# Starting addresses of the expert stage's tiles: a right-end spacer of 480 bytes, and two small tensors joined to others

## The chip, the cores and the metric

One core of one Trainium2 chip. The metric is device microseconds of the whole program, the median of several runs. A run of the same program is repeated to within some tenths of a per cent; three runs of the kernel before gave 1493.5, 1497.95 and 1489.89 us.

## The reference

A decoder layer on x of 8 batches x 256 tokens x 512 features, float32:

```python
x = x + attn(layernorm(x))            # 16 heads, keys masked to 26 first and 64 last positions
x = x + long_conv(ctx, ctx, layernorm(x), ssm_kernel, D)   # 32 heads of 8 x 8 products, causal convolution
x = x + moe(layernorm(x))
# moe: E = 12 experts, top 3 of a softmax router, 512 -> 1280 -> 512
for e in range(E):
    sel = top_idx == e; mask = sel.any(-1)
    w_e = sum(where(sel, ew, 0)) / max(sel.sum(), 1)
    h = relu(x @ w1[e] + b1[e]);  h = h @ w2[e] + b2[e]
    out = out + mask * (w_e * h)
phi = sigmoid(relu(out.mean(axis=1) @ Wp1 + bp1) @ Wp2 + bp2)
return out * (1.0 - (phi > 0.7) * 0.8)
```

Inputs and outputs are float32. Products are made of three float32r matmuls each: every factor is split in a rounded high part and a low part, and hi*hi + hi*lo + lo*hi is summed.

## The kernel before, in words

The program runs four functions one after the other: `attention` (0 to some 300 us), `convolution` (to some 494 us), `route` (to some 523 us) and `experts` (to the end). Each has one instruction stream per engine, in an order written out by hand, tied together by semaphores. No planner takes part.

`route` sorts the 2048 x 3 pairs of token and expert into NTILE = 59 tiles of 128 tokens, so that each tile belongs to one expert, and leaves tables: `gidx` (rows to gather), `sidx` (rows to add to), `wt`, `eid`, `tstart_i`, `wexp`. Meanwhile the first expert's weights arrive in `w_lo` by four DMAs and ScalarE rounds them into `w_hi`.

`experts` goes through the 59 tiles. For a tile, GpSimd gathers 128 rows of the normalised x from DRAM (`gather`, L1797 to L1800, into `xg`; the first two, L1849 and L1852, stand before the loop), TensorE transposes them (L1947), ScalarE and GpSimd make `xf`, `xh`, `xl` (L1877, L1878, L1806), TensorE makes the first product in column chunks of 512, 512 and 256 (L1962, L1963, L1967: `ps_h`), ScalarE copies it to `h` (L1884), TensorE transposes it (L1975), ScalarE applies bias and relu into `h` and rounds into `hh` (L1893, L1897), GpSimd makes `hl` (L1810), TensorE makes the second product (L1985, L1986, L1989: `ps_y`), ScalarE scales into `y` (L1903), GpSimd adds the bias (L1820) and adds the rows to `acc` in DRAM by an indirect DMA (L1835). TensorE's order for a tile is: transposes of h, first product of the next tile, transposes of x for the tile after that, second product.

The weights of the next expert are loaded beside this by SyncE in 20 chunks of [128, 512] into the four buffers of `stage` (L1640), and VectorE splits each into `w_hi` and `w_lo` (L1685, L1687). Before each half of the chunks VectorE waits for TensorE's last use of the buffer and does a one-column addition into `turn` (L1728, L1732). GpSimd does such one-column additions into columns 0 to 4 of `tick` (`settle`, L1794).

At the end SyncE reads the sums of all tiles but two back from `acc` (L1666, four DMAs of 1 MB), VectorE adds them in pairs (L1752) and TensorE pools them (L1996); when the last tile is added, eight DMAs of 512 KB fetch `acc` (L1671), VectorE combines (L1783) and eight DMAs store (L1675).

All operands of this stage lie in SBUF at addresses that follow from the order of allocation. A tile on the left side begins where the one before it ended, rounded up to 32 bytes; a tile on the right side is laid downwards from 229344. By that arithmetic the byte addresses within a partition are these, with the remainder by 512 in brackets: `gidx` 19616 (160); `si` 22912, `tick` 22944, `turn` 22976, `b1_now` 23008; `xf` 23072 (32), `xh` 25120 (32), `xl` 27168 (32), `h` 29216 (32), `hh` 34336 (32), `hl` 39456 (32), `y` 44576 (32), ending at 48672; from the right `w_hi` 147424 (480), `w_lo` 65504 (480), `stage` 57312 (480), `b2_sb` 53216 (480), `gi` 53184 (448), `xg` 49088 (448). In `attention` the weights `wq_hi` to `wo_lo` begin at remainder 384, and `xs` and `qe` too; the transposed rows that its matmuls load beside them begin at 0 (`xT_hi` 176640, `xT_lo` 180736) and at 416 (`oT_hi` 215456, `oT_lo` 217504). Every row, chunk and buffer inside these tiles is a multiple of 512 bytes long where TensorE or a DMA starts a run in it, so that the remainder is the same for all of them.

Of the kernel before, what the change touches and what calls it, by code (L numbers as in the profile page):

```python
# [6 lines left out]
F32 = mybir.dt.float32  # L7
# [3 lines left out]
U32 = mybir.dt.uint32  # L11
ACT = mybir.ActivationFunctionType
ALU = mybir.AluOpType
AX_X = mybir.AxisListType.X

P = 128
B, S, D = 8, 256, 512
# [32 lines left out]
NTILE = NT * TOPK + (E * (P - 1)) // P  # L50
# [1489 lines left out]
def experts(nc, cst, w_hi, w_lo, stage, stage_in, split_done, wcat, b2, b2_sb, b2_in, b2_ready, b1_sb, xnd, x2d, x2,  # L1540
# [6 lines left out]
    gidx, sidx, wt, eid, tstart_i, wexp = tabs  # L1547
    gi, xg, gi_ready, g_in = first
    tile_f, cnt, ps_t = book
    o, o_in, end_small, small_in = end  # L1550
    with ExitStack() as ctx:
        def sb(name, shape, dt=F32):
            return ctx.enter_context(nc.sbuf_tensor(name, shape, dt))
# [4 lines left out]
        def sem(name):  # L1558
            return ctx.enter_context(nc.semaphore(name))

        si = sb("si", [P, 2], U32)
        tick = sb("tick", [P, 5])
        turn = sb("turn", [P, 1])
        b1_now = sb("b1_now", [P, KF])
        xf = sb("xf", [P, KD * P])
        xh = sb("xh", [P, KD * P], F32R)
# [51 lines left out]
        tabs_ready = sem("tabs_ready")  # L1618
# [60 lines left out]
        def _(dve):  # L1679
# [14 lines left out]
            v = nc.vector  # L1694
# [3 lines left out]
            expert, used_, tok_, to_ = (tile_f[:, i] for i in range(4))  # L1698
# [3 lines left out]
            note(v.tensor_scalar(tok_, m_tile, float(P), -1.0, ALU.mult, ALU.add))  # L1702
            note(v.tensor_tensor(tok_, tok_, m_place, ALU.add))
            note(v.tensor_scalar(tok_, tok_, 0.0, None, ALU.max))
            v.tensor_copy(gidx[:], tok_).then_inc(tabs_ready, 1)
            dve.wait_ge(gi_ready, 2)
            lower(0)
            lower(1)
# [16 lines left out]
                lower(q)  # L1725
            with dve.Fori(1, E) as e:
                dve.wait_ge(h_done, first_tile(dve, e - 1, 3))
                nc.vector.tensor_tensor(turn[:], cst[:, 0:1], cst[:, 0:1], ALU.add)  # L1728
                for c in range(N1):
                    split(e, c)  # L1730
                dve.wait_ge(y_done, first_tile(dve, e - 1, 1))
                nc.vector.tensor_tensor(turn[:], cst[:, 0:1], cst[:, 0:1], ALU.add)  # L1732
                for c in range(N1, NCHUNK):
                    split(e, c)
                dve.wait_ge(b2_in, 16 * e + 16)
                b2_w = view(b2_sb[:], (e % 2) * D, [[1, D]])
                nc.vector.tensor_tensor(b2_w, b2_w, view(wexp[:], e, [[0, D]]), ALU.mult).then_inc(b2_ready, 1)
# [313 lines left out]
def decoder_layer(nc, out, **a):  # L2051

    with ExitStack() as ctx:
        def sb(stack, name, shape, dt=F32):
            return stack.enter_context(nc.sbuf_tensor(name, shape, dt))

        cst = sb(ctx, "cst", [P, NCONST])
        tabs = (sb(ctx, "gidx", [P, NTILE], U32), sb(ctx, "sidx", [P, NTILE], U32), sb(ctx, "wt", [P, NTILE]),
                sb(ctx, "eid", [1, NTILE], I32), sb(ctx, "tstart_i", [1, E], I32), sb(ctx, "wexp", [P, E]))
        b1_sb = sb(ctx, "b1_sb", [P, E * KF])  # L2060
        kpad = nc.dram_tensor("kpad", (SH, KPAD), F32, kind="Internal").ap()
        x2d = nc.dram_tensor("x2d", (NT * P, D), F32, kind="Internal").ap()
        xnd = nc.dram_tensor("xnd", (NT * P, D), F32, kind="Internal").ap()
        acc = nc.dram_tensor("acc", (NT * P + P, D), F32, kind="Internal").ap()
        with ExitStack() as mid:
            ranked = (sb(mid, "prob", [P, NT, E]), sb(mid, "rank", [P, NT, E]), sb(mid, "col", [P, 2, NT]))
            with ExitStack() as early:
                xs = sb(early, "xs", [P, NT, D])
                qe = sb(early, "qe", [P, LB * B * SH * CH])
                dve_step = ctx.enter_context(nc.semaphore("dve_step"))  # L2070
                exps = [ctx.enter_context(nc.semaphore(n)) for n in ("exp_in", "exp_out")]
                count = [0]

                def moved(steps=None):
                    if steps is not None:
                        count[0] = steps.base + steps.n
                    return count[0]

                front = sb(early, "front", [P, (TPB + 8) * D])
                n_kv, n_cc = LB * B * NPAIR, LB * B * CE  # L2080
                sizes = [n_kv] * AHEAD + [n_cc] * 2 + [D] * AHEAD
                parts = [front[:, sum(sizes[:i]):sum(sizes[:i + 1])] for i in range(len(sizes))]
                ahead = (parts[AHEAD + 2:], parts[AHEAD:AHEAD + 2], parts[:AHEAD],
                         [early.enter_context(nc.semaphore(f"toe_in{i}")) for i in range(NTOE)],
                         [early.enter_context(nc.semaphore(f"cc_in{i}")) for i in range(2)],
                         early.enter_context(nc.semaphore("kv_ready")))
                attention(nc, xs, cst, a["x"], a["L0_attn_Wq"], a["L0_attn_Wk"], a["L0_attn_Wv"], a["L0_attn_Wo"],
                          a["L0_attn_bq"], a["L0_attn_bk"], a["L0_attn_bv"], a["L0_attn_bo"], a["consts"], qe,
                          a["L0_xattn_ssm_kernel"], a["L0_xattn_D"], kpad, a["ctx_rev"], front, ahead, dve_step, moved)
                res = sb(early, "res", [P, LB * B * S])  # L2090
                convolution(nc, xs, cst, qe, res, a["ctx_rev"], kpad, ranked, a["L0_ffn_Wr"], a["L0_ffn_br"],
                            a["L0_ffn_b1"], b1_sb, x2d, xnd, acc, ahead, dve_step, moved, exps)
            with ExitStack() as late:
                w_hi = late.enter_context(nc.sbuf_tensor("w_hi", [P, 2, WS], F32R, side="right"))
                w_lo = late.enter_context(nc.sbuf_tensor("w_lo", [P, 2, WS], F32R, side="right"))
                x2_in = late.enter_context(nc.semaphore("x2_in"))
                x2 = w_hi[:, 0, 0:NT * D].bitcast(F32).rearrange("p (t d) -> p t d", d=D)
                o = w_lo[:, 0, 0:NT * D].bitcast(F32).rearrange("p (t d) -> p t d", d=D)
                spare = w_lo[:, 0, NT * D:WS].bitcast(F32)
                wp1, bp1, wp2, bp2 = (a[f"L0_ffn_{n}"] for n in ("Wp1", "bp1", "Wp2", "bp2"))  # L2100
                PH = wp1.shape[1]
                KP = PH // P
                gate = (spare[:, 0:KD * PH].rearrange("p (k n) -> p k n", k=KD), spare[:, KD * PH:KD * PH + KP],
                        spare[:, KD * PH + KP:KD * PH + 2 * KP], spare[:, KD * PH + 2 * KP:KD * PH + 2 * KP + 1])
                end_small = ((gate[0], wp1.rearrange("(k p) n -> p k n", p=P)), (gate[1], bp1), (gate[2], wp2),
                             (gate[3], bp2.partition_broadcast(P)))
                end = (o, [late.enter_context(nc.semaphore(f"o_in{b}")) for b in range(B)], end_small,
                       late.enter_context(nc.semaphore("small_in_e")))
                with ExitStack() as busy:
                    def right(name, shape, dt=F32):  # L2110
                        return busy.enter_context(nc.sbuf_tensor(name, shape, dt, side="right"))

                    stage = right("stage", [P, NSTAGE, WC])
                    b2_sb = right("b2_sb", [P, 2, D])
                    stage_in = [busy.enter_context(nc.semaphore(f"stage_in{i}")) for i in range(NSTAGE)]
                    split_done = busy.enter_context(nc.semaphore("split_done"))
                    b2_in = busy.enter_context(nc.semaphore("b2_in"))
                    b2_ready = busy.enter_context(nc.semaphore("b2_ready"))
                    first = (right("gi", [P, 2], U32), right("xg", [P, 2, D]), busy.enter_context(nc.semaphore("gi_ready")),
                             [busy.enter_context(nc.semaphore(f"g_in{i}")) for i in range(2)])  # L2120
                    book = (view(stage[:], 0, [[NTILE, 4], [1, NTILE]]), view(stage[:], 4 * NTILE, [[E, 6], [1, E]]),
                            busy.enter_context(nc.psum_tensor("ps_td", [P, 3, 512], F32)))
                    route(nc, cst, ranked, w_hi, w_lo, a["wcat"], a["L0_ffn_b2"], b2_sb, b2_in, first, tabs, book, dve_step, moved, exps)
                    experts(nc, cst, w_hi, w_lo, stage, stage_in, split_done, a["wcat"], a["L0_ffn_b2"], b2_sb, b2_in,
                            b2_ready, b1_sb, xnd, x2d, x2, x2_in, acc, first, end, gate, out, tabs, book, dve_step, moved)
# [55 lines left out]
```

## Time and profile before

| | |
|---|---|
| median of three runs | 1493.5 us |
| profiled execution, its time | 1495.83 us |
| profiled execution, its span | 1494.1 us |
| TensorE busy, share of the span | 1379.5 us, 92% |
| GpSimd busy | 842.6 us, 56% |
| VectorE busy | 819.8 us, 55% |
| ScalarE busy | 698.1 us, 47% |
| mean granted clock of TensorE | 0.953 |

The busy time of TensorE says only that a matmul was in flight, since they overlap. The chain of work that ended last tells which of them set the time, and the table by stretches tells where the engine had nothing to do. PE is TensorE, DVE VectorE, ACT ScalarE, POOL GpSimd, SP SyncE; a q behind the name is the engine's sequencer, which issues DMAs.

### The profile page before, as it was taken

What the parts mean: (1) busy time and instruction counts of PE and PEld (TensorE: products, weight loads), DVE (VectorE), ACT (ScalarE), POOL (GpSimd) and SP (SyncE); (2) the same over time, 40 slices, a digit from 0 to 9 for tenths busy, and PEclk for the clock granted to TensorE, in tenths of its full rate; (3) what the DMA queues carried; (4) which work ended last, traced back from release to release, by engine and by line L of the source; (5) the groups of instructions that cost most, each with busy time, mean ns of one, the idle gap of its engine ahead of it and who ended that gap; (6) DMA issues with size and microseconds to landing.
All of it is one profiled execution on the core that took longest, in us unless ns stands there. A gap on an engine that the chain in (4) does not pass through costs nothing.

```text
span 1494.1 us, 27777 instructions
## 1 busy us (share of the span) xinstructions
PE 1379.5 (92%) x7868; PEld 1135.9 (76%) x7869; DVE 819.8 (55%) x1197; ACT 698.1 (47%) x1878; POOL 842.6 (56%) x955
## 2 busy tenths in 40 slices
PE   5899998799986279999999999999999999999994
PEld 3777776577765268888888888888888888888883
DVE  6788887599997884745264444647444452000013
ACT  3657666244554234454444544445444454444530
POOL 0456445244653067767576676767766666565640
PEclk9999998899997589999999999999999999999985
DMA  7000000253333335545254344445444443151146
GB/s 268 1 1 0 0 0 26 82 188 97 111 99 136 153 115 126 147 113 137 66 148 105 106 106 111 124 113 156 107 111 95 123 112 77 35 154 35 31 132 232
DMA packets 77576, 152.42 MB, mean 102 GB/s; under 512 B 9120, under 2 KB 13728, under 8 KB 77024
## 3 DMA queue, kind: packets, MB, share of 16 engines
q1 hardware_dynamic: 62496, 115.09, 24.2%
q0 software_dynamic: 14320, 35.40, 12.0%
q10 hardware_dynamic: 720, 1.44, 0.3%
q8 instruction: 21, 0.34, 0.1%
q14 instruction: 19, 0.16, 0.0%
HBM read 119.31 MB, written 32.59 MB: 102 GB/s over the span
## 4 chain that ended last, share of the span: by engine, by line
PE 62%; DMA 2%; DVE 0%; SPq 0%; issue 0%; ACT 0%; DVEq 0%; POOL 0%; POOLq 0%
PE ps_h L1962 9%; PE ps_h L1967 9%; PE ps_h L1963 9%; PE ps_y L1985 9%; PE ps_y L1986 9%; PE ps_y L1989 9%; PE ps_td L1975 4%; PE ps_xd L1947 2%; DMA w_lo<-acc 1%; PE ps_xd L1996 0%; DMA xg<-xnd,gi 0%; DMA acc<-y,si 0%; DVE w_lo L1783 0%; SPq L1671 0%; DVE w_lo L1752 0%
## 5 line engine op out<-in xcount | busy, mean ns | idle before, releaser
L1962 PE MATMUL ps_h<-w_hi,xh 128*128 x708 | 251.5, 367 | 1.5 <-ACT xh L1878 1.4
L1963 PE MATMUL ps_h<-w_lo,xh 128*128 x708 | 244.3, 356 | 0.0
L1687 DVE TENSOR_TENSOR w_lo<-stage,w_hi 128x512 f32 x220 | 226.6, 1030 | 28.6 <-DVE w_hi L1685 2.9
L1985 PE MATMUL ps_y<-w_hi,hh 128*128 x590 | 238.8, 405 | 0.0
L1986 PE MATMUL ps_y<-w_lo,hh 128*128 x590 | 233.6, 396 | 0.0
L1820 POOL TENSOR_TENSOR y<-y,b_sb 128x512 f32<-128x512 f32 x58 | 79.7, 1374 | 226.6 <-ACT y L1903 226.6
L1810 POOL TENSOR_TENSOR hl<-h,hh 128x1280 fp32r<-128x1280 f32 x59 | 180.9, 3067 | 17.9 <-ACT hh L1897 17.5
L1903 ACT ACTIVATE y<-ps_y,wt 128x512 f32<-128x512 f32 x59 | 40.6, 688 | 293.5 <-PE ps_y L1989 293.5
L1884 ACT ACTIVATE h<-ps_h 128x512 f32<-128x512 f32 x177 | 80.7, 527 | 196.5 <-POOL hl L1810 185.6
L1967 PE MATMUL ps_h<-w_hi,xl 128*128 x708 | 166.7, 357 | 0.0
L1893 ACT ACTIVATE h<-ps_td,b_now 128x128 f32<-128x128 f32 x590 | 159.0, 392 | 3.9 <-PE ps_td L1975 1.2
L1962 PEld LDWEIGHTS ps_h<-w_hi,xh 128*128 128x128 f32 x708 | 133.9, 189 | 24.5 <-issue 2.1
L1963 PEld LDWEIGHTS ps_h<-w_lo,xh 128*128 128x128 f32 x708 | 134.0, 189 | 20.3
L1989 PE MATMUL ps_y<-w_hi,hl 128*128 x590 | 147.5, 395 | 0.0
L1728 DVE TENSOR_TENSOR turn<-cst 128x1 f32<-128x1 f32 x11 | 2.7, 242 | 253.6 <-PE ps_h L1967 253.6
L1967 PEld LDWEIGHTS ps_h<-w_hi,xl 128*128 128x128 f32 x708 | 120.6, 188 | 21.4
L1989 PEld LDWEIGHTS ps_y<-w_hi,hl 128*128 128x128 f32 x590 | 110.3, 187 | 27.3
L1985 PEld LDWEIGHTS ps_y<-w_hi,hh 128*128 128x128 f32 x590 | 111.4, 189 | 24.9
L1986 PEld LDWEIGHTS ps_y<-w_lo,hh 128*128 128x128 f32 x590 | 111.3, 189 | 24.8
L1685 DVE CAST w_hi<-stage 128x512 f32 x220 | 126.5, 575 | 5.2 <-DMA stage<-in_wcat 4.3
L1835 POOL DMA_INDIRECT acc<-y,si x59 | 101.1, 1714 | 29.4 <-issue 14.9
L1742 DVE COPY xf<-w_lo 128x256 f32<-128x256 f32 x1 | 0.3, 295 | 181.3 <-POOL xl L1806 181.3
(256 smaller groups left out, 2647.6 us busy)
## 6 DMA issues: line engine op xcount, KB each, us to landing
stage<-in_wcat SPq DMA_DIRECT2D x220, 256.0 KB, 3.0
front<-in_ctx_rev SPq DMA_DIRECT2D x32, 192.0 KB, 2.4
w_lo<-in_wcat SPq DMA_DIRECT2D x4, 1280.0 KB, 11.7
acc<-added_c POOLq DMA_DIRECT2D x1, 4352.0 KB, 17.4
front<-kpad SPq DMA_DIRECT2D x16, 256.0 KB, 3.4
toe<-kpad SPq DMA_DIRECT2D x16, 256.0 KB, 3.6
x2d<-xs SPq DMA_DIRECT2D x16, 256.0 KB, 2.4
xnd<-xn_c SPq DMA_DIRECT2D x16, 256.0 KB, 2.0
```

Of the source, the lines that this page charges most:

```text
L1685: nc.vector.tensor_copy(hi, stage[:, c % NSTAGE]).then_inc(w_rounded, 1)
L1687: nc.vector.tensor_tensor(lo, stage[:, c % NSTAGE], hi.bitcast(F32), ALU.subtract).then_inc(split_done, 1)
L1810: nc.gpsimd.tensor_tensor(hl[:], h[:], hh[:].bitcast(F32), ALU.subtract).then_inc(hl_ready, 1)
L1835: pool.indirect_dma_start(acc, bass.IndirectOffsetOnAxis(ap=si[:, par:par + 1], axis=0), y[:, par], None, compute_op=ALU.add).then_inc(add ...
L1884: nc.scalar.activation(h[:, lo:hi], ps_h[:, c, 0:hi - lo], ACT.Copy).then_inc(h_evac, 1)
L1893: last = nc.scalar.activation(h[:, k * P:(k + 1) * P], ps_t[:, k // 4, (k % 4) * P:(k % 4 + 1) * P], ACT.Relu, bias=b1_now[:, k:k + 1])
L1962: nc.tensor.matmul(out, x_hi, part(w_hi, e, k * FF + lo, hi - lo), start=(k == 0), stop=False)
L1963: nc.tensor.matmul(out, x_hi, part(w_lo, e, k * FF + lo, hi - lo), start=False, stop=False)
L1967: last = nc.tensor.matmul(out, xl[:, k * P:(k + 1) * P], part(w_hi, e, k * FF + lo, hi - lo), start=False, stop=(k == KD - 1))
L1985: nc.tensor.matmul(ps_y[:], h_hi, part(w_hi, e, KD * FF + k * D, D), start=(k == 0), stop=False)
L1986: nc.tensor.matmul(ps_y[:], h_hi, part(w_lo, e, KD * FF + k * D, D), start=False, stop=False)
L1989: last = nc.tensor.matmul(ps_y[:], hl[:, k * P:(k + 1) * P], part(w_hi, e, KD * FF + k * D, D), start=False, stop=(k == KF - 1))
```

## The change

A tensor `tail` of 120 float32 (480 bytes) that nothing uses is allocated first on the right side, so that all below it moves down by 480 bytes. `gi` becomes the last two columns of `gidx`, and `turn` the sixth column of `tick`. The rows of `gidx` and `tick` still take 256 and 32 bytes, so nothing on the left side ahead of `tick` moves. By the same arithmetic: `b1_now` 22976, `xf` 23040 (0), `xh` 25088 (0), `xl` 27136 (0), `h` 29184 (0), `hh` 34304 (0), `hl` 39424 (0), `y` 44544 (0), ending at 48640; `w_hi` 146944 (0), `w_lo` 65024 (0), `stage` 56832 (0), `b2_sb` 52736 (0), `xg` 48640 (0); `gi` at 19852. No instruction, wait, loop or DMA is added or taken away, and none changes its shape.

```diff
-        tick = sb("tick", [P, 5])
-        turn = sb("turn", [P, 1])
+        tick = sb("tick", [P, 6])
+        turn = tick[:, 5:6]
...
-            v.tensor_copy(gidx[:], tok_).then_inc(tabs_ready, 1)
+            v.tensor_copy(gidx[:, 0:NTILE], tok_).then_inc(tabs_ready, 1)
...
-                nc.vector.tensor_tensor(turn[:], cst[:, 0:1], cst[:, 0:1], ALU.add)     # L1728, L1732
+                nc.vector.tensor_tensor(turn, cst[:, 0:1], cst[:, 0:1], ALU.add)
...
-        tabs = (sb(ctx, "gidx", [P, NTILE], U32), sb(ctx, "sidx", [P, NTILE], U32), sb(ctx, "wt", [P, NTILE]),
+        tabs = (sb(ctx, "gidx", [P, NTILE + 2], U32), sb(ctx, "sidx", [P, NTILE], U32), sb(ctx, "wt", [P, NTILE]),
...
             with ExitStack() as late:
+
+                late.enter_context(nc.sbuf_tensor("tail", [P, 120], F32, side="right"))
                 w_hi = late.enter_context(nc.sbuf_tensor("w_hi", [P, 2, WS], F32R, side="right"))
...
-                    first = (right("gi", [P, 2], U32), right("xg", [P, 2, D]), ...
+                    first = (tabs[0][:, NTILE:NTILE + 2], right("xg", [P, 2, D]), ...
```

## Rows read from the trace of the kernel before

**Rows 1.** The page's chain of work that ended last, by engine and by line.
```profile
PE 62%; DMA 2%; DVE 0%; SPq 0%; issue 0%; ACT 0%; DVEq 0%; POOL 0%; POOLq 0%
```
**Rows 2.** Stretches: us, then busy us of PE, PEld, DVE, ACT, POOL, clock, DMA share, GB/s.
```profile
300.00:520.00 220.00, 176.93 (x876) 139.99 (x874) 203.67 (x243) 104.91 (x167) 94.06 (x118) 0.89 0.39 131
600.00:800.00 200.00, 200.00 (x1032) 167.66 (x1031) 94.99 (x127) 91.46 (x229) 136.57 (x154) 1.00 0.46 117
1200.00:1400.00 200.00, 200.00 (x1032) 167.64 (x1032) 31.32 (x43) 91.99 (x229) 124.39 (x153) 1.00 0.33 80
```
**Rows 3.** The chain in order of time, experts' loop: start us, us, what.
```profile
555.87 2.34 PE ps_y L1989 x10
571.42 2.34 PE ps_y L1989 x10
...
1426.48 2.34 PE ps_y L1989 x10
```
**Rows 4.** Waits from 545 to 1420 us: engine, line, releaser: total, times, longest.
```profile
DVE turn L1728 <- PE ps_h L1967: 253.6, 10, 37.5
DVE turn L1732 <- PE ps_y L1989: 63.5, 10, 6.4
DVE w_hi L1685 <- DMA stage<-in_wcat: 1.3, 3, 0.6
```
**Rows 5.** Timeline of PE, one tile of the experts: start us, us, what.
```profile
809.75 1.10 PE L1967 MATMUL ps_h<-w_hi,xl 128*128 x4
810.68 0.40 PE L1962 MATMUL ps_h<-w_hi,xh 128*128 x1
...
814.42 0.63 PE L1967 MATMUL ps_h<-w_hi,xl 128*128 x4
814.89 0.60 PE L1947 MATMUL ps_xd<-cst,xg 128*128 128x128 f32 x4
```
**Rows 6.** Timeline of PE in the attention stage.
```profile
157.12 1.09 PE L745 MATMUL bank<-wo_hi,oT_lo 128*128 128x512 f32 x4
158.05 0.60 PE L715 MATMUL bank<-cst,front 128*128 128x128 f32 x4
...
163.14 1.09 PE L745 MATMUL bank<-wq_hi,xT_lo 128*128 128x512 f32 x4
164.07 1.91 PE L782 MATMUL bank<-cst,pm 128*90 128x128 f32 x16
```
**Rows 7.** Timeline of all engines, the last but one tile.
```profile
1432.74 1.27 ACT L1897 ACTIVATE hh<-h 128x1280 fp32r<-128x1280 f32 x1
1434.09 2.95 POOL L1810 TENSOR_TENSOR hl<-h,hh 128x1280 fp32r<-128x1280 f32 x1 [0.65 <-ACT hh L1897]
1436.76 0.39 PE L1985 MATMUL ps_y<-w_hi,hh 128*128 x1
1441.42 2.50 PE L1989 MATMUL ps_y<-w_hi,hl 128*128 x10
```
**Rows 8.** Timeline around the first gather.
```profile
524.39 3.66 POOL L1852 DMA_INDIRECT xg<-xnd,gi  x1 [0.29 <-POOL gi L1849]
528.36 2.24 POOL L1852 DMA_INDIRECT xg<-xnd,gi  x1 [0.30 <-issue]
```
**Rows 9.** The chain in order of time, its DMA pieces behind 520 us.
```profile
524.39 6.07 DMA xg<-xnd,gi
...
1437.41 8.24 DMA w_lo<-acc
...
1464.79 4.92 DMA acc<-y,si
...
1472.18 8.67 DMA w_lo<-acc
1480.87 3.41 DVE w_lo L1783 x5
```
**Rows 10.** DMA issues of the end: count, KB each, median us to landing.
```profile
w_lo<-acc SPq DMA_DIRECT2D x8, 512.0 KB, 6.6
out<-w_lo SPq DMA_DIRECT2D x8, 512.0 KB, 9.1
```
**Rows 11.** Stretches with the DMA engines near full (columns as in Rows 2).
```profile
0.00:30.00 30.00, 14.49 (x72) 10.84 (x77) 19.85 (x38) 11.30 (x17) 1.59 (x8) 0.96 0.92 331
1472.00:1481.00 9.00, 0.57 (x3) 0.47 (x3) 7.79 (x16) 0.21 (x1) 0.00 (x0) 0.50 1.03 385
1484.00:1492.00 8.00, 0.00 (x0) 0.00 (x0) 0.94 (x2) 0.00 (x0) 0.00 (x0) 0.50 1.05 408
```
**Rows 12.** Timeline of PE where its clock had fallen, second product of the last tile.
```profile
1453.15 0.77 PE L1985 MATMUL ps_y<-w_hi,hh 128*128 x1
1457.53 0.40 PE L1985 MATMUL ps_y<-w_hi,hh 128*128 x1
```

More of the change, by code:

```diff
@@ L1731, in _ @@
                 dve.wait_ge(y_done, first_tile(dve, e - 1, 1))
-                nc.vector.tensor_tensor(turn[:], cst[:, 0:1], cst[:, 0:1], ALU.add)
+                nc.vector.tensor_tensor(turn, cst[:, 0:1], cst[:, 0:1], ALU.add)
                 for c in range(N1, NCHUNK):
@@ L2118, in decoder_layer @@
                     b2_ready = busy.enter_context(nc.semaphore("b2_ready"))
-                    first = (right("gi", [P, 2], U32), right("xg", [P, 2, D]), busy.enter_context(nc.semaphore("gi_ready")),
+                    first = (tabs[0][:, NTILE:NTILE + 2], right("xg", [P, 2, D]), busy.enter_context(nc.semaphore("gi_ready")),
                              [busy.enter_context(nc.semaphore(f"g_in{i}")) for i in range(2)])
```

## The prediction, made before the changed kernel was run

> **What bounds the kernel now.** I read the page's chain of work first, then the table by stretches, then the chain in order of time, and last the timelines of single tiles. The page's chain gives TensorE by far the largest share, 62%, and all DMAs together 2% [rows 1]. The stretches show why: from 600 to 800 us TensorE is busy for 200.00 of 200 us at granted clock 1.00, and so it is again from 1200 to 1400 us, while VectorE, ScalarE and GpSimd have room; before 520 us it is not full [rows 2]. The reader is to see in the chain by time that this loop has one fixed beat: the ten matmuls of L1989 begin at 555.87 us, at 571.42 us and so on to 1426.48 us [rows 3], which is 56 beats in 870.61 us, 15.546 us a tile, with nothing between two tiles. So for 59 tiles x 15.546 = 917 us of the 1494.1 us span only TensorE's own pace counts. The other engines wait for it, not it for them: VectorE waited 253.6 + 63.5 us for the weight buffers to come free, and 1.3 us in all for the weights' DMAs [rows 4].
>
> **The places that the change can reach.** Nothing moves in SBUF before the routing stage: the longer rows of `gidx` still take 256 bytes, so every address of attention and convolution stays, and the first 494 us are the same program on the same addresses. From there on no instruction is added or removed. What changes is the start of each run inside its line of 512 bytes: 480 becomes 0 for the weights, the staging buffers and the two bias rows, 448 becomes 0 for the gathered rows, 32 becomes 0 for x, h and y. I take the readers and writers one by one.
>
> **TensorE's moving operand.** A matmul of 512 columns streams 2048 bytes of w_hi or w_lo. Its pace is read from starts: four of them last from 809.75 to 810.68 us, 0.93 us [rows 5], 233 ns each. At 2.4 GHz (granted clock 1.00) 512 columns at one a cycle are 213 ns, so 20 ns of each are something else, and if that were the ragged start of the run the change could take it away. The upper bound of such a gain is large: 24 + 30 matmuls of 512 columns a tile x 20 ns + 12 of 256 columns x 10 ns = 1.2 us a tile, 71 us over 59 tiles. The value I take is 0, for two reasons. First, the attention stage streams the same 2048 bytes from remainder 384, a multiple of 128, where the experts' 480 is a multiple of 32 alone: four of its matmuls go from 157.12 to 158.05 us, 0.93 us too [rows 6]. A line of 64 or 128 bytes that had to be fetched once more would show between the two, and doesn't. Second, the 256-column matmuls take 814.89 - 814.42 = 0.47 us for four [rows 5], half of the 0.93; a run of 2048 bytes that starts at 480 touches 5 lines of 512 bytes and one of 1024 touches 3, so a price by the line touched would give 0.6 of it (0.56 with lines of 256), not 0.5. The extra 20 ns go with the columns and not with the lines. The lower bound, a loss, is treated as a rival below.
>
> **Stationary operand, ScalarE, VectorE and GpSimd.** These read and write x, h, w and stage from the new starts. Where they got faster or slower in the loop, it would be covered. hh is ready at 1432.74 + 1.27 = 1434.01 us and first used at 1436.76 us: 2.75 us of cover for a 1.27 us instruction. hl is ready at 1437.04 and used at 1441.42 us: 4.4 us of cover for 2.95 us [rows 7]. VectorE's two waits above, up to 37.5 us long, are its cover [rows 4]. So I cost all this at nothing, in both directions; without that cover each 0.1 us of a slower hh or hl would be 59 x 0.1 = 6 us.
>
> **turn in tick.** The same 20-odd one-column additions, written 20 bytes behind GpSimd's columns instead of in their own 32 bytes. They stand after VectorE's waits and its cover holds for them [rows 4]: nothing.
>
> **gi in gidx.** The index copies and the gathers read the same words at 19852 instead of 53184. In the loop a gather is asked for nearly two tiles before its rows are transposed. On the path is the first alone: 6.07 us from issue to landing [rows 9], of which GpSimd's own work is 3.66 us, against 2.24 us for the second, which is the same instruction once more [rows 8]. I know no row for an index at an address of another remainder; the spread of these two, 1.4 us, is what I allow on either side, and I take 0, as only the address of the index word differs and everything else that GpSimd does stays.
>
> **DMA rows.** All rows that the expert stage moves are 2048 bytes on the SBUF side (10240 for the first weights). In the loop they are hidden: the DMA engines are 0.46 full and the weights arrive before VectorE asks [rows 2, 4]. On the path are 6.07 us (first gather), 8.24 us (early sums), 4.92 us (the last tile's add) and the end, from 1472.18 us to the end of the span, 21.9 us, in which 4.2 MB are read and 4.2 MB stored [rows 9, 10]: together 41.1 us. What alignment is worth there I bound by the stretches in which the engines are full. At the start of the program, with SBUF remainder 384, the engines moved 331 GB/s at share 0.92, or 360 per full share; at the end, with remainder 480, 385 at 1.03 and 408 at 1.05, or 374 and 389 [rows 11]. The start of the run inside its line doesn't show in the price of a byte. Were the whole end to run at the better of its own two rates, 8.39 MB / 408 GB/s = 20.6 us, that is 1.3 us less; the same 6% on the other 19.2 us gives 1.1 us more. So the gain is between 0 and 2.4 us; a loss by the same rows could not be above the step from 408 to 385, 2.4 us. I take -0.7 us, nearer to nothing, since the two remainders compared cost the same.
>
> The Trainium skill speaks for more here. Its page "DMA: Bandwidth & Descriptors", section "How a descriptor splits into AXI transactions", says that a descriptor which doesn't start on 256 bytes is read from the boundary below, and the bytes before its start cost beats of 32 bytes. 480 lies 224 above such a boundary, 7 beats on 64 for 2048 bytes. By that the sum of this part would be up to -4 us, as an estimate from the page. By the same rule remainder 384 would cost 4 beats on 64 and the start of the program should have had the better rate; the rows show the reverse, 360 against 374 and 389 [rows 11], so I hold to them.
>
> **What follows a faster end of the loop.** While TensorE waits for the early sums it falls to half clock: the matmuls of the last second product are 0.77 us at 1453.15 and 0.40 us at 1457.53 us [rows 12]. If the early sums came 0.5 us earlier, that stretch would begin earlier too but last as long; I count nothing for it. At best the fall doesn't happen, which would save about 2 us: ten matmuls took the 4.38 us between these two starts, where ten at full clock take 2.33 us.
>
> **Sum.** -0.7 us, on the profiled execution 1495.83 - 0.7 = 1495.1 us. Its time stands 2.3 us above the median 1493.5, within the spread of the three runs (1489.89 to 1497.95), so the forecast for a median is 1493.5 - 0.7 = 1492.8 us. The likeliest case alone, with all DMA, gather and clock bounds, is 1493.5 - 2.4 - 1.4 - 2 = 1487.7 to 1493.5 + 2.4 + 1.4 = 1497.3 us. A difference of less than 0.5%, 7.5 us, is about what a measurement of this kernel can't tell from no change.
>
> **Rivals.** (a) *Lines of 512 bytes do set TensorE's pace.* For it: 233 ns is not 213 ns, and no row of before streams from remainder 0, so that the case proper isn't in the trace. Against it: rows 5 and 6 as above. If a run loses one of its 5 line fetches and these set the 20 ns, a fifth of 71 us goes: 14 us, 1479 us; if all goes, 1422 us. Chance 0.05.
> (b) *Everything starts in step, and collides.* This is the one that ends slower. Before, w began at remainder 480, x and h at 32, stage at 480, xg at 448; after, all at 0. If TensorE's two reads (the weights' stream and the next stationary load) meet in the same part of SBUF at each start, every matmul of the loop waits a little: there are 66 a tile x 59 = 3894. From 2 ns each it is 7.8 us and measurable; at 4 ns, which is 2% of 233 ns, 15.6 us: 1508 us. For it: nothing in the profile, except that the engine is full and hides nothing. Against it: in attention the weights at 384 run beside stationary tiles at 416 (oT_lo, 157.12 to 158.05 us) and at 0 (xT_lo, 163.14 to 164.07 us), and both take 0.93 us [rows 6], so the distance between the two reads has not mattered yet. Chance 0.05.
> (c) *A ragged start costs the DMA engines time*, and the fall of the clock is avoided. The three full stretches differ in price by 8% (360 to 389 per full share [rows 11]); if alignment gives that much on all of the 41.1 us it is 3.3 us, and 2 us for the clock: 1493.5 - 5.3 = 1488.2 us. For it: the engines are full at the end, so there it counts whole. Against it: the stretch at 480 is the cheaper one. This is the case in which the skill's rule on descriptors, weighed above, would be right. It ends on the edge of what can be told. Chance 0.10, half of it beyond 0.5% by the chance of measurement.
> (d) *The tiles don't land on the lines as said*, because an allocation is rounded otherwise than I worked out. Then nothing changes at all: 1493.5 us. Chance 0.03; it doesn't differ in time from the forecast.
>
> **Chances and range.** The forecast (with d) 0.80, c 0.10, a 0.05, b 0.05. Faster by over 0.5%: a, half of c, and 0.01 of the forecast's own spread: 0.11. Slower: b and 0.01 more: 0.06. Within: 0.83. The range of the forecast, 1487.7 to 1497.3 us, widened by about 1 us for the spread between medians, is 1486.5 to 1498.5 us; it takes in c and leaves out a and b.
>
> **What would show it.** The beat of L1989 should stay 15.55 us, and four matmuls of L1967 0.93 us apart from start to start; a beat of 15.3 would be (a), one above 15.6 would be (b). The loop's stretches should stay 200.00 of 200 us. The end from the first fetch of the sums to the end of the span should be 21 to 22 us; under 20 us would be (c). VectorE's and GpSimd's means may move by some per cent with no effect on the span. My forecast is wrong if TensorE's pace depends on 256 or 512 bytes in a way that no row of before can show.

## The result: 1% faster, and all of it is TensorE's own pace

The changed kernel takes 1477.88 us (median of 4 runs, 1477.21 to 1478.54) where the one before took 1493.8 (4 runs, 1489.89 to 1497.95). The ratio is 0.9897, 95% interval 0.9878 to 0.9916: 15.9 us less, outside the forecast's 1486.5 to 1498.5. Two later comparisons on other chips gave 0.9879 (0.9860 to 0.9897) and 0.9896 (0.9878 to 0.9913). The profiled execution took 1478.1 us with a span of 1476.3 us, 17.8 us below the span of before.

The table by stretches (columns as in [rows 2]) looks as before: TensorE full at clock 1.00. What differs is the count of its matmuls in the same 200 us, 1048 for 1032.

```profile
300.00:520.00 220.00, 176.64 (x875) 139.75 (x873) 203.54 (x243) 104.90 (x167) 94.13 (x118) 0.89 0.39 131
...
600.00:800.00 200.00, 200.00 (x1048) 171.00 (x1047) 100.08 (x131) 93.83 (x234) 141.13 (x159) 1.00 0.48 119
```

The chain in order of time gives the beat, which answers to [rows 3], and the DMAs behind the loop, which answer to [rows 9].

```profile
524.25 6.11 DMA xg<-xnd,gidx
555.51 2.27 PE ps_y L1989 x10
570.77 2.27 PE ps_y L1989 x10
...
1410.44 2.27 PE ps_y L1989 x10
...
1421.20 7.69 DMA w_lo<-acc
...
1446.78 4.61 DMA acc<-y,si
...
1454.96 10.67 DMA w_lo<-acc
```

From the first of these L1989 to the last are 56 beats in 854.93 us, 15.267 us a tile for 15.546. That is 15.7 us of the 17.8. Ahead of 555 us the two differ by 0.36 us. From the last L1989 shown to the end of the span it is 65.9 us for 67.6, the other 1.7 us. These 1.7 us are not shown to come from the change: in two later profiles of the same changed kernel the same piece takes 67.4 and 66.3 us, while the beat is 15.267 us in both.

The timeline of TensorE in one tile (start, duration, instruction) shows which matmuls got faster. To be read are the starts.

```profile
793.18 0.28 PE L1962 MATMUL ps_h<-w_hi,xh 128*128 x1
...
794.61 0.60 PE L1947 MATMUL ps_xd<-cst,xg 128*128 128x128 f32 x4
...
802.89 0.48 PE L1962 MATMUL ps_h<-w_hi,xh 128*128 x1
...
805.72 0.39 PE L1962 MATMUL ps_h<-w_hi,xh 128*128 x1
...
807.54 1.07 PE L1967 MATMUL ps_h<-w_hi,xl 128*128 x4
808.44 0.28 PE L1962 MATMUL ps_h<-w_hi,xh 128*128 x1
```

Twelve matmuls of 512 columns take 808.44 - 805.72 = 2.72 us, 227 ns each; before, four took 0.93 us, 233 ns [rows 5]. The four of L1967 alone take 0.90 us. The 256-column matmuls got a little slower: the twelve from 793.18 to the transposes of x at 794.61 take 1.43 us, where in the kernel before, from 797.93 to 799.35, they took 1.42 us:

```profile
797.93 0.28 PE L1962 MATMUL ps_h<-w_hi,xh 128*128 x1
...
799.35 0.60 PE L1947 MATMUL ps_xd<-cst,xg 128*128 128x128 f32 x4
```

The weight loads of L1989 kept their length, 187 ns at the least.

### The profile page after: what moved, and what is told of

Read it like the earlier page. It is cut to its first block, busy times and chain, and to the rows that moved or that the text cites. A ratio compares the mean times of both kernels' runs of the same rounds, so it can differ in the third digit from the quotient of the medians.

```text
span 1476.3 us, 27777 instructions
## 1 busy us (share of the span) xinstructions
PE 1360.4 (92%) x7868; PEld 1134.8 (77%) x7869; DVE 827.6 (56%) x1197; ACT 698.2 (47%) x1878; POOL 845.6 (57%) x955
## 4 chain that ended last, share of the span: by engine, by line
PE 61%; DMA 2%; DVE 0%; SPq 0%; issue 0%; ACT 0%; DVEq 0%; POOL 0%; POOLq 0%
PE ps_h L1962 9%; PE ps_h L1963 9%; PE ps_h L1967 9%; PE ps_y L1985 9%; PE ps_y L1986 9%; PE ps_y L1989 9%; PE ps_td L1975 4%; PE ps_xd L1947 2%; DMA w_lo<-acc 1%; DMA xg<-xnd,gidx 0%; DMA acc<-y,si 0%; PE ps_xd L1996 0%; SPq L1671 0%; DVE w_lo L1752 0%; DVE w_lo L1783 0%
## 5 line engine op out<-in xcount | busy, mean ns | idle before, releaser
L1986 PE MATMUL ps_y<-w_lo,hh 128*128 x590 | 231.5, 392 | 0.0
L1687 DVE TENSOR_TENSOR w_lo<-stage,w_hi 128x512 f32 x220 | 214.4, 974 | 28.6 <-DVE w_hi L1685 2.9
L1967 PE MATMUL ps_h<-w_hi,xl 128*128 x708 | 164.1, 354 | 0.0
L1685 DVE CAST w_hi<-stage 128x512 f32 x220 | 142.8, 649 | 6.9 <-DMA stage<-in_wcat 6.2
L1989 PE MATMUL ps_y<-w_hi,hl 128*128 x590 | 143.5, 389 | 0.0
L1728 DVE TENSOR_TENSOR tick<-cst 128x1 f32<-128x1 f32 x11 | 3.4, 312 | 240.2 <-PE ps_h L1967 240.2
L1967 PEld LDWEIGHTS ps_h<-w_hi,xl 128*128 128x128 f32 x708 | 121.2, 189 | 18.4
L1989 PEld LDWEIGHTS ps_y<-w_hi,hl 128*128 128x128 f32 x590 | 110.8, 188 | 23.0
L1806 POOL TENSOR_TENSOR xl<-xf,xh 128x512 fp32r<-128x512 f32 x59 | 77.7, 1316 | 38.1 <-ACT xh L1878 37.4
```

The source lines that it names most:

```text
L1685: nc.vector.tensor_copy(hi, stage[:, c % NSTAGE]).then_inc(w_rounded, 1)
L1687: nc.vector.tensor_tensor(lo, stage[:, c % NSTAGE], hi.bitcast(F32), ALU.subtract).then_inc(split_done, 1)
L1967: last = nc.tensor.matmul(out, xl[:, k * P:(k + 1) * P], part(w_hi, e, k * FF + lo, hi - lo), start=False, stop=(k == KD - 1))
L1986: nc.tensor.matmul(ps_y[:], h_hi, part(w_lo, e, KD * FF + k * D, D), start=False, stop=False)
L1989: last = nc.tensor.matmul(ps_y[:], hl[:, k * P:(k + 1) * P], part(w_hi, e, KD * FF + k * D, D), start=False, stop=(k == KF - 1))
```

## The experiments

The theories. **M**: the start of the moving run (the weights' row, streamed through the array) sets the pace. **S**: the start of the stationary tile does (the rows of x or h, loaded before each matmul). **C**: the other engines' accesses to SBUF disturbed TensorE less. Later **B**, both starts must lie on a line of 256 bytes, and **D**, only the distance between the two starts counts, by its remainder by 256. A pair (r, s) means: moving run at r, stationary tile at s, both in bytes behind a line of 512; its distance is r less s.

### TensorE alone, swept over the two starts

```python
for i in range(48):
    nc.tensor.matmul(ps[:, g, 0:512], part(st, s, 128, i % 8), part(mv, r, 512, i % 8),
                     start=(i == 0), stop=(i == 47))     # one such line for each pair (r, s)
```

> Leaves the whole decoder layer out: TensorE alone runs 29 groups of 48 float32r matmuls, each with a weight load, on constants, every other engine idle; groups differ in the byte offsets of the moving run (0 to 480 behind a line of 512) and of the stationary tile (0, 32, 256) and in the columns (512, 384, 256, 128). Theory M (the start of the moving run sets TensorE's pace by itself): 512 columns from 0 take about 227 ns from start to start, from 480 about 233 ns, whatever the stationary tile's start; 256 columns about 119 and 116 ns; the other offsets tell how long the line is. Theory S (the stationary tile's start sets it): groups differ with the stationary tile's start, 0 against 32, and not with the moving run's. Theory C (the kernel's gain is less contention with the other engines' accesses): all groups of 512 columns take the same, near 227 ns or less.

The timeline merges the 48 matmuls of a line. The step is the difference of two starts, by 48. The lines are: 49 the pair (0, 0), 50 (32, 0), 51 (64, 0), 53 (128, 0), 55 (256, 0), 59 (480, 0), 60 (0, 32), 61 (480, 32), which is the kernel before.

```profile
24.39 11.04 PE L49 MATMUL ps<-mv,st 128*128 128x512 f32 x48
35.27 11.37 PE L50 MATMUL ps<-mv,st 128*128 128x512 f32 x48
46.47 11.16 PE L51 MATMUL ps<-mv,st 128*128 128x512 f32 x48
57.47 11.37 PE L52 MATMUL ps<-mv,st 128*128 128x512 f32 x48
68.68 11.36 PE L53 MATMUL ps<-mv,st 128*128 128x512 f32 x48
79.88 11.36 PE L54 MATMUL ps<-mv,st 128*128 128x512 f32 x48
91.08 11.06 PE L55 MATMUL ps<-mv,st 128*128 128x512 f32 x48
101.97 11.17 PE L56 MATMUL ps<-mv,st 128*128 128x512 f32 x48
...
135.34 11.36 PE L59 MATMUL ps<-mv,st 128*128 128x512 f32 x48
146.53 11.35 PE L60 MATMUL ps<-mv,st 128*128 128x512 f32 x48
157.72 11.35 PE L61 MATMUL ps<-mv,st 128*128 128x512 f32 x48
168.91 11.09 PE L62 MATMUL ps<-mv,st 128*128 128x512 f32 x48
```

(35.27 - 24.39) / 48 = 226.7 ns at (0, 0); 233.3 at (32, 0); 229.2 at (64, 0); 233.3 at (128, 0); 226.9 at (256, 0); 233.1 at (480, 0) and at (480, 32). With every other engine idle (480, 32) and (0, 0) differ by 6.4 ns, as 233 and 227 ns do in the two kernels, so C isn't needed. Line 60, the stationary tile at 32 under a moving run at 0, takes 233.1 ns too: either start can spoil it, and M alone falls.

### Only the weights on their line

```diff
-        tick = sb("tick", [P, 6])
-        b1_now = sb("b1_now", [P, KF])
+        tick = sb("tick", [P, 16])
+        b1_now = tick[:, 6:6 + KF]        # x, h and y begin at remainder 480
```

> Right side as after (w_hi, w_lo, stage, xg at 0), left side moved to 480 (xf, xh, xl, h, hh, hl, y), by joining b1_now to tick. Theory M: the beat of a tile stays 15.27 us, about 1478 us. Theory S: back to 15.55 us, about 1494 us. Theory C: between the two or at the old beat.

1492.97 us (10 runs), ratio 1.0000, interval 0.9987 to 1.0014. The chain by time has the old beat, 725.91 - 710.37 = 15.54 us:

```profile
710.37 2.33 PE ps_y L1989 x10
...
725.91 2.33 PE ps_y L1989 x10
```

The right side is where the change put it, and nothing of the gain is left. M is refuted in the kernel as well. The DMAs into stage and xg are aligned here, and the time is that of before.

### Only x and h on their line

```diff
-                late.enter_context(nc.sbuf_tensor("tail", [P, 120], F32, side="right"))
```

> Without the spacer of 480 bytes: left side as after (x and h at 0), right side at 480 as before. Theory M: beat 15.55 us, about 1494 us. Theory S: beat 15.27 us, about 1478 us. Theory C: in between.

1493.91 us (10 runs), ratio 1.0003, interval 0.9989 to 1.0016; the beat is 15.54 us.

```profile
709.25 2.33 PE ps_y L1989 x10
...
724.79 2.33 PE ps_y L1989 x10
```

S falls too. Since this kernel also holds both joins, `gi` in `gidx` and `turn` in `tick`, it shows that they cost and bring nothing beyond that interval.

### The weights at 256

```diff
-                late.enter_context(nc.sbuf_tensor("tail", [P, 120], F32, side="right"))
+                late.enter_context(nc.sbuf_tensor("tail", [P, 56], F32, side="right"))
```

> Spacer of 224 bytes in place of 480: w_hi, w_lo, stage and xg at 256, x and h at 0. Theory M with lines of 256 bytes or less: beat 15.27 us, 1478 us. Theory M with lines of 512 bytes: beat near 15.55 us, 1494 us. Theory S: 15.27 us.

1476.78 us (4 runs), ratio 0.989, interval 0.9867 to 0.9912, the full gain. The period is not 512: a distance of 256 is as good as 0.

### Both starts together

> Leaves the decoder layer out, as the sweep before it: TensorE alone, 35 groups of 48 matmuls. Theory B (both starts count by their remainder by 256 bytes; the pace is fast only when both are near 0): 512 columns from 0 with a stationary tile at 64, 96, 128, 192 take 229 to 233 ns, at 256 take 227 ns; equal remainders (32, 32), (64, 64), (128, 128) take 229 to 233 ns too. Theory D (the distance between the two starts counts, not each): the equal ones take 227 ns. For the groups with a stationary tile of 32 columns B says nothing; if the weight load's reads are what disturbs, the start of the tile should matter less there. bfloat16 (half the bytes) and plain float32 (half the pace) should show less than 1 ns or nothing, if the pace of reading is the limit.

Same program, other pairs. Lines: 64 the pair (32, 32), 65 (64, 64), 66 (128, 128), 67 (192, 192), 68 (64, 32), 69 (64, 128), 70 (128, 64).

```profile
119.05 11.08 PE L64 MATMUL ps<-mv,st 128*128 128x512 f32 x48
129.97 11.07 PE L65 MATMUL ps<-mv,st 128*128 128x512 f32 x48
140.87 11.08 PE L66 MATMUL ps<-mv,st 128*128 128x512 f32 x48
151.79 11.09 PE L67 MATMUL ps<-mv,st 128*128 128x512 f32 x48
162.72 11.36 PE L68 MATMUL ps<-mv,st 128*128 128x512 f32 x48
173.91 11.36 PE L69 MATMUL ps<-mv,st 128*128 128x512 f32 x48
185.11 11.36 PE L70 MATMUL ps<-mv,st 128*128 128x512 f32 x48
196.31 11.35 PE L71 MATMUL ps<-mv,st 128*128 128x512 f32 x48
```

227.5, 227.1, 227.5 and 227.7 ns where the starts are equal but on no line of 256; 233.1, 233.3 and 233.3 where they differ. At distance 0 that is D, and B falls. The pair (0, 192) has 229.0 ns as (64, 0) has 229.2: the same distance, 64. But (128, 64), at distance 64 too, has 233.3 ns (line 70). So D is right in that distance 0 is fast wherever it was tried, and is not the whole rule for the other distances.

Plain float32 takes 858.3 ns with the moving run at 0 and at 128 under a tile at 0. That is 3.8 times as long as float32r takes, not twice as the expectation had it, and no step. bfloat16 takes 215.8 ns at (128, 0), (0, 32) and (128, 32), and 215.7 at (0, 0): no step either, as expected. In the group of (0, 0), line 82, the first of the 48 records is missing, so that the difference of the starts is divided by 47:

```profile
292.05 10.31 PE L82 MATMUL ps<-mb,sb 128*128 128x512 bf16 x47
302.19 10.52 PE L83 MATMUL ps<-mb,sb 128*128 128x512 bf16 x47
```

The groups with 32 stationary columns take 231.5 and 230.6 ns for moving runs at 0 and 128 under a tile at 0, so distance 0 isn't the faster one there, and 239.0 ns at (0, 32).

### The weights at 64

```diff
-                late.enter_context(nc.sbuf_tensor("tail", [P, 120], F32, side="right"))
+                late.enter_context(nc.sbuf_tensor("tail", [P, 104], F32, side="right"))
```

> Spacer of 416 bytes: w_hi, w_lo, stage and xg at 64, x and h at 0. The sweep had 229.2 ns for 512 columns from 64, against 226.7 from 0, and 118 against 120 for 256 columns. Theory B: the beat of a tile goes from 15.27 to 15.27 + 54 x 0.0025 - 12 x 0.002 = 15.38 us, the time to 1478 + 59 x 0.11 = 1484.5 us. A rule of all or nothing at 256 bytes says 15.55 us and 1494 us.

1480.54 us (4 runs), ratio 0.9901, interval 0.9879 to 0.9924; the changed kernel beside it had 1476.88 us (6 runs).

```profile
554.26 2.29 PE ps_y L1989 x10
...
569.59 2.29 PE ps_y L1989 x10
```

The beat is 15.33 us: between the two, as the sweep's 229.2 ns asks, and not at 15.55. It is 0.06 us a tile above the changed kernel where I worked out 0.11; 59 x 0.06 = 3.5 us, and the medians lie 3.7 us apart.

### Nothing on a line, distance 0

```diff
-        tick = sb("tick", [P, 6])
-        b1_now = sb("b1_now", [P, KF])
+        tick = sb("tick", [P, 16])
+        b1_now = tick[:, 6:6 + KF]
...
-                late.enter_context(nc.sbuf_tensor("tail", [P, 120], F32, side="right"))
```

> No tensor of the expert stage on a line of 512: no spacer, b1_now joined to tick, so that w_hi, w_lo, stage and xg begin at 480 and x, h and y at 480 too: distance 0. Theory D: as fast as the changed kernel, beat 15.27 us, about 1478 us, 0.989 of before. Theory B: beat 15.55 us, about 1494 us.

1481.16 us (4 runs), ratio 0.9911, interval 0.9891 to 0.9931; the changed kernel beside it had 1478.24 us (4 runs).

```profile
557.17 2.27 PE ps_y L1989 x10
...
572.46 2.27 PE ps_y L1989 x10
```

This decides it. Both edits were made above, one at a time, and each gave the old time; here w, x and h all begin at 480, none on a line, and the kernel has the pace of the change: beat 15.29 us, ten matmuls of L1989 in 2.27. It is 2.9 us slower than the changed kernel, of which the beat explains 59 x 0.02 = 1.2; the rest is open, and the two intervals against before (0.9878 to 0.9913 for the changed kernel) overlap.

### Finer distances

> Leaves the decoder layer out: TensorE alone, groups of 48 float32r matmuls, stationary tile at 0, moving run at 4 to 256 bytes behind it, and one pair at (300, 44). Theory D (only the distance moving start less stationary start, by its remainder by 256, sets the pace): 512 columns take 227 ns at distance 0 and 256 and for (300, 44), 229 at 64, 233 at 32, 96 to 224; the finer steps tell how near to 0 it must be (4, 16, 240). 256 columns: 120 at 0, and 3 ns or so less at some of the others. Theory B (both starts must be on a line) says 233 for (300, 44).

Lines: 57 distance 4, 58 distance 16, 70 distance 240, 71 distance 256, 72 the pair (300, 44).

```profile
40.47 11.48 PE L57 MATMUL ps<-mv,st 128*128 128x512 f32 x48
51.80 11.28 PE L58 MATMUL ps<-mv,st 128*128 128x512 f32 x48
62.91 11.36 PE L59 MATMUL ps<-mv,st 128*128 128x512 f32 x48
...
185.61 11.05 PE L70 MATMUL ps<-mv,st 128*128 128x512 f32 x48
196.50 11.08 PE L71 MATMUL ps<-mv,st 128*128 128x512 f32 x48
207.42 11.21 PE L72 MATMUL ps<-mv,st 128*128 128x512 f32 x48
218.47 11.07 PE L73 MATMUL ps<-mv,st 128*128 128x512 f32 x48
```

236.0 ns at distance 4, 231.5 at 16, 226.9 at 240 and 227.5 at 256. The pair (300, 44), at distance 256 but with both starts off the 16 bytes, takes 230.2 ns: off 16 bytes D isn't the whole rule at distance 256 either. The pair (480, 32), which is the kernel before, takes 233.1 once more. With 256 columns distance 0 is the slowest, 119.8 ns, and others behind a tile at 0 take 117.9 to 119.6; (480, 32) takes 113.7 ns, in both sweeps, though (192, 0) is at the same distance and takes 117.9. For 256 columns D doesn't hold.

### Attention too

```diff
+                sb(early, "lead", [P, 32])     # ahead of xs
...
+        sb("gap_x", [P, 32])                   # ahead of xT_hi
...
+        sb("gap_o", [P, 24])                   # ahead of oT_hi
```

> The changed kernel, and 128 bytes of spacer ahead of xs, 128 ahead of xT_hi and 96 ahead of oT_hi, so that in attention the weights begin at 0 and the transposed rows at 256. Theory B: four matmuls of L745 (of Wq and Wo) 0.91 us apart in place of 0.93; 6.4 ns on 48 matmuls x 8 batches is 2.5 us at most, where TensorE is the bound: 1475.5 to 1478 us. The theory that only the expert stage's other engines were disturbed says no change of that pace.

1474.99 us (5 runs), ratio 0.9867, interval 0.9849 to 0.9886; the changed kernel beside it 1476.88 us (6 runs, 0.9879). In attention four matmuls on Wq are now 131.75 - 130.84 = 0.91 us apart; before it was 0.93 [rows 6].

```profile
130.84 1.07 PE L747 MATMUL bank<-wq_hi,xT_lo 128*128 128x512 f32 x4
131.75 1.91 PE L784 MATMUL bank<-cst,pm 128*90 128x128 f32 x16
```

The intervals against before overlap, so that 1.9 us less is as expected, but not shown by the times; the pace is.

With the key rows in rows of 128 columns as well (and the spacer ahead of oT_hi longer, so that it stays at remainder 0 by 256):

```diff
-        xkh, xkl = (sb(n, [P, KD, NK], F32R) for n in ("xkT_hi", "xkT_lo"))
+        xkh, xkl = (sb(n, [P, KD, P], F32R) for n in ("xkT_hi", "xkT_lo"))
...
-                hi, lo = ([... c[:, k] ...])
+                hi, lo = ([... c[:, k, 0:NK] ...])
...
-        sb("gap_o", [P, 24])
+        sb("gap_o", [P, 40])
```

> The attention spacers of the earlier variant, and the transposed key rows xkT in rows of 128 columns in place of 90, so that each of their four tiles too is at distance 0 from Wk and Wv. Theory D: 24 more matmuls a batch at 0.227 in place of 0.233 us, 1.2 us over 8 batches where TensorE is the bound: 1474 us.

The changed kernel ran beside each of the two, first beside the one without the key rows, then beside this one:

> The changed kernel once more, for comparison on this chip: 1478 us, 0.989 of before.

> The changed kernel once more, for comparison on this chip with the variant beside it: about 1477.5 us.

1476.67 us (4 runs), ratio 0.9884, interval 0.9867 to 0.9901, and the changed kernel 1478.24 (4 runs, 0.9896). The expected 1474 us was missed, and the step of 0.227 us that it counted on did not come: the key rows' matmuls, whose stationary tiles have 90 columns, are at distance 0 by the layout, and four of them still take 143.13 - 142.20 = 0.93 us.

```profile
142.20 1.09 PE L747 MATMUL bank<-wv_hi,xkT_lo 128*90 128x512 f32 x4
143.13 1.03 PE L784 MATMUL bank<-cst,pm 128*90 128x128 f32 x8
```

No version is shown to beat the change; the two with attention in step were 1.6 and 1.9 us below it on their chips.

## Why the prediction was wrong

**The bound** was read rightly: TensorE's pace in the expert loop alone decides, and 59 tiles carry every nanosecond of it to the end. The lever, 54 matmuls of 512 columns a tile, was named as well. What the change removes of each is 6.4 ns (233.1 to 226.7, TensorE alone), a third of the 20 ns that I had as the bound: 54 x 6.4 = 346 ns a tile. Measured: 0.279 us. Where it comes from, the starts of the whole tiles of the loop in the two traces say (53 before, 54 after, means): the 24 matmuls of 512 columns of the first product went from 5677 to 5553 ns, its 12 of 256 columns from 1414 to 1433, the 30 of the second product from 7092 to 6918, the 14 transposes from 1364 to 1363. So the 512-column matmuls gave 298 ns of the 346, and the 256-column ones took 19 back.

**The step that failed** is "TensorE's moving operand", where the value taken was 0. The argument compared the loop with attention, saw 0.93 us in both and concluded that the start of a run doesn't matter. It varied the wrong thing. By the layout, the experts' pair (480, 32) is at distance 192, attention's two pairs (384, 416) and (384, 0) at 224 and 128 [rows 5, 6]. All three are slow distances (233.3, 233.1 and 233.3 ns in the sweeps), and 0 was nowhere in the trace. Three equal values at three slow distances are no evidence for a fourth, as rival (a) half said; the text gave it 0.05 nevertheless. The second argument, that half the columns take half the time and so no line is paid for, was right for lines, but took for granted that a gain could come by lines alone.

**Rival (b)** named what counts, the distance between the starts of TensorE's two operands, with the sign turned round: starting in step is the fast case. It gave 2 to 4 ns of loss for 6.4 ns of gain. That the two reads get in each other's way, as it supposed, is not shown by any run. The argument against it, "the distance between the two reads has not mattered yet", is the same mistake.

**Rival (a)** came nearest in time, 1479 us for 1477.88, but by luck, for a reason that the runs refute: with nothing on a line the kernel is as fast in its beat, and with the weights alone on lines it isn't.

**ScalarE, VectorE, GpSimd, the joins**: right. VectorE still waits 240.2 and 56.9 us for free buffers in the loop, for [rows 4]'s 253.6 and 63.5, and the kernel with both joins, its weights still at 480, gave 1.0003.

**DMA**: no effect is shown, and the -0.7 us is too small to be told from none. The full stretches at the end (columns as in [rows 2]) hardly moved:

```profile
1454.96:1463.00 8.04, 0.00 (x0) 0.00 (x0) 7.65 (x13) 0.00 (x0) 0.00 (x0) 0.50 1.01 376
1464.00:1472.00 8.00, 0.00 (x0) 0.00 (x0) 2.39 (x4) 0.00 (x0) 0.00 (x0) 0.50 1.05 408
```

376 and 408 GB/s at remainder 0, for 385 and 408 at 480 [rows 11], and the kernel with aligned DMAs and unaligned x took 1493.0 us, with an interval that reaches to 0.9987 of before, 1.9 us less. The rule of the Trainium skill, "DMA: Bandwidth & Descriptors", section "How a descriptor splits into AXI transactions", by which the bytes between a 256-byte boundary and a start behind it still cost beats, by the prediction's estimate up to 4 us here, does not show. The first gather took 6.11 us for 6.07. From the first fetch of the sums to the end of the span it is 21.3 us for 21.9. Behind the last L1989 shown the three profiles of the changed kernel have 65.9, 67.4 and 66.3 us, so the 1.7 us of the first are no more than their spread.

**The range** was built round the forecast's small terms, and left out a bound of 71 us on the strength of one comparison. A term that is multiplied by 3186 matmuls and rests on a case the trace doesn't contain should have been kept in it.

## What to carry to other kernels

Where TensorE alone is the bound, ask where the moving run and the stationary tile start relative to each other, not whether each is aligned: for float32r with 512 columns and 128 stationary ones, and starts on 32 bytes, equal remainders by 256 bytes are worth 6 ns, 3%, of each matmul, and one spacer and a join gave it here. With 90 or 32 stationary columns, with 256 moving ones and with bfloat16 or float32 no such gain was seen. Measure such a thing with TensorE alone, one profile with a line for each case, before arguing from rows that all lie on the same side. And a constant that is the same in every row of a trace may only mean that every row has the same fault.

## What the runs showed of the hardware that was not expected

- The step of 512-column float32r matmuls with a weight load each, TensorE alone at 2.4 GHz (granted clock 1.00), by distance of the starts: 226.7 to 227.7 ns at 0 and 256, 226.9 at 240, 229.0 to 229.4 at 64 (but 233.3 for the pair (128, 64)), 230.0 to 231.5 at 16, 48, 80 and 112, 232.1 to 234.2 at 32, 96, 128, 160, 192 and 224, 234.8 at 208, 236.0 at 4. Why the distance counts, no run shows.
- The gain doesn't scale with the columns: it is 6.4 ns at 512 and a loss at 256 (119.8 against 117.9 ns at distances 32, 64 and 192 from a tile at 0, and 113.7 for the pair (480, 32)); 384 columns take 173.3 ns at distance 0 and at 192 (175.0 at 0 in the first sweep), 128 columns 110.4 and 111.7.
- bfloat16 with 512 columns takes 215.7 to 215.8 ns at all four pairs tried, float32 858.3 at both; neither shows a step.
- In the changed kernel the first matmuls of a product are slower than the rest. By the means of the same 54 tiles, the 2nd to 12th of the first product lie 228.9 ns apart and the 2nd to 4th of the second 231.7, where later ones have 226.7; before, the same ones were 233.0 and 233.3 apart, like the rest. The 298 ns that the 512-column matmuls gave fall short of 346 mainly by this; its cause is open.
